# Embedding, state-space mixing and routed experts on one core: the order of every engine's steps given as lists

## The reference, cut to what matters

```python
h = patches(x) @ W_proj + b_proj + pos_emb            # 32 x 36 tokens
h = concatenate([h, weights[positions(x_txt)]])       # 32 x 68 tokens, 256 wide
# attention stand-in: projections, gate, convolution, a linear scan over the 68 tokens, then
out = einsum('blh,dh->bld', y, W_out) + b_out         # y: 512 wide
h = h + layernorm(xn + out, ln_g, ln_b)               # xn = layernorm(h)
# feed-forward: x2 = layernorm(h), top 2 of 4 experts
g = softmax(layernorm(x2, rn_g, rn_b) @ router_w.T)
hid = relu(layernorm(x2 @ w1[e], ln_g[e], ln_b[e]))   # 512 wide
out = sum over the 2 experts of (hid @ w2[e]) * weight
h = h + layernorm(out, on_g, on_b)
```

## Time and profile before

| | |
|---|---|
| median of the runs | 492.49 us |
| the profiled execution: time, span | 492.58 us, 490.8 us |
| from the output projections to the last block (226 to 460 us) | 234 us |
| from there to the end | 31 us |
| granted clock of TensorE, mean | 0.957 |

### The profile page before, as it was taken

How to read it: one execution, slowest core, us unless ns; L and a number is a source line. 1 busy time by engine, 2 the same in 40 slices (tenths; PEclk the granted TensorE clock), 3 DMA queues, 4 the chain that set the end, 5 groups by cost and what they waited for, 6 DMA issues and landing times.

```text
span 490.8 us, 9987 instructions
## 1 busy us (share of the span) xinstructions
PE 431.7 (88%) x3149; PEld 363.0 (74%) x3149; DVE 334.1 (68%) x981; ACT 295.2 (60%) x667; POOL 156.3 (32%) x261
## 2 busy tenths in 40 slices
PE   7879999799899999999989789999999999999400
PEld 5769977567688878787877667888878888888300
DVE  6886576688999325335887877857665666565584
ACT  2854468277966465226654455876786777877351
POOL 6000000000000000002253887764778644553322
PEclk9999999799999999989989999999999999999855
DMA  8982099700039742964411322222322333252252
GB/s 177 190 230 58 33 320 325 230 0 2 1 77 256 183 115 67 240 212 140 140 45 54 100 83 68 98 87 67 109 98 77 109 108 110 75 148 79 94 198 83
DMA packets 58734, 59.94 MB, mean 122 GB/s; under 512 B 25368, under 2 KB 51260, under 8 KB 57404
## 3 DMA queue, kind: packets, MB, share of 16 engines
q1 hardware_dynamic: 54236, 48.68, 37.0%
q0 software_dynamic: 3552, 9.74, 5.3%
q10 hardware_dynamic: 896, 0.89, 0.7%
HBM read 34.50 MB, written 24.80 MB: 121 GB/s over the span
## 4 chain that ended last, share of the span: by engine, by line
PE 57%; DVE 12%; issue 10%; POOL 8%; ACT 8%; DMA 3%; SPq 1%; POOLq 0%; DVEq 0%; ACTq 0%
PE bank L1047 12%; PE bank L884 9%; PE bank L434 8%; PE bank L436 7%; PE bank L435 7%; POOL sorted_x L674 3%; PE bank L1033 3%; PE bank L904 3%; PE bank L958 2%; POOL h L709 1%; DMA expert_y<-ysb,toid 1%; PE bank L1015 1%; DMA got<-expert_y 1%; ACT U L471 1%; DVE spj L1408 1%
## 5 line engine op out<-in xcount | busy, mean ns | idle before, releaser
L1047 PE MATMUL bank<-w,hr 128*128 x320 | 75.8, 380 | 1.1 <-DVE ysb L1670 0.6
L1047 PEld LDWEIGHTS bank<-w,hr 128*128 128x128 f32 x320 | 60.1, 190 | 11.1 <-issue 2.1
L647 POOL MEMSET ones<- 128x128 f32 x1 | 0.2, 209 | 204.9 <-PE bank L919 204.9
L1241 ACT ACTIVATE hr<-bank,gsel 128x128 f32<-128x128 f32 x160 | 59.9, 461 | 0.0
L722 POOL DMA_INDIRECT expert_y<-ysb,toid x40 | 42.8, 1070 | 50.6 <-DVE ysb L1670 30.6
L884 PE MATMUL bank<-Tb,U 68*32 68x68 f32 x1024 | 45.4, 354 | 0.3 <-issue 0.3
L884 PEld LDWEIGHTS bank<-Tb,U 68*32 68x32 f32 x1024 | 40.1, 140 | 3.6 <-issue 3.0
L1655 DVE BATCH_NORM_STATS2 bsth<-bank 128x6 f32<-128x512 f32 x40 | 27.7, 693 | 20.1 <-PE bank L436 19.8
L674 POOL DMA_INDIRECT sorted_x<-x2s,slot x34 | 33.6, 987 | 14.9 <-issue 9.7
L1233 ACT ACTIVATE hn<-bank,nmrh,rsh 128x512 f32<-128x512 f32 x40 | 31.1, 778 | 11.5 <-DVE nmrh L1664 9.9
L434 PE MATMUL bank<-w_hi,bT_hi 128*128 x80 | 35.0, 438 | 0.2 <-issue 0.2
(11 more groups left out here) (304 smaller groups left out, 1169.6 us busy)
## 6 DMA issues: line engine op xcount, KB each, us to landing
Tb<-ssm_kernels SPq DMA_DIRECT2D x16, 680.0 KB, 7.3
sorted_x<-zpad SPq DMA_DIRECT2D x6, 1419.0 KB, 13.3
xg<-sorted_x SPq DMA_DIRECT2D x40, 129.0 KB, 2.1
got<-expert_y SPq DMA_DIRECT2D x17, 256.0 KB, 4.3
XI<-in_x_dram SPq DMA_DIRECT2D x12, 288.0 KB, 5.6
h0r<-h_spill SPq DMA_DIRECT2D x17, 128.0 KB, 2.1
out_dram<-acc SPq DMA_DIRECT2D x17, 128.0 KB
...
```

The lines of the kernel that those rows point to most:

```text
L1047: mm = pe.matmul(bank[second_bank(i)][:, 0:D], hr[:, i % 3, c, :], w2[:, bass.ds(expert[i], 1), c, :].rearrange("p o n -> p (o n)"), start ...
L1241: last = act.activation(hr[:, i % 3, c, :], bank[3 + i % 2][:, c * P:(c + 1) * P], ACT.Relu, scale=gsel[:, i, 0, c:c + 1], bias=gsel[:, i, ...
```

## The change

The numbers and `place_of` are gone. Each engine has a string, one letter for a step; the k-th occurrence of a letter is index k of its kind (`w1s` and all others run upward in index). Operations, waits, buffers and `fill` are the same; every engine has the same set of steps as before in another sequence.

```diff
-        RUN = 0.1
-        HEAD = PARTS[0].stop // 2
-        STARTS = dict(tiles=((-228.34, 36.22), (-51.95, 71.10)), blocks=((49.05, 19.06), (417.37, 19.11)),
-                      sums=((579.34, 113.82), (1443.32, 34.88)))
...
-            "dve": dict(out=-176.0, ln1a=-146.8, ln1b=-131.0, h1a=-113.1, x2=-95.4, c1=-68.1, c2=0.8, lg=-50.7,
...
-            t0, dt = STARTS["sums" if kind in SUMS else "tiles"][int(n >= HEAD)]
-            return t0 + (n - HEAD if n >= HEAD else n) * dt + AT[who][kind] + (late * AT["odd"][kind] if late else 0)
...
-            return sorted(steps, key=lambda s: place_of(who, *s))
+        NAMES = {
+            "pe": dict(y="yT", o="out", x="x2T", l="lgm", r="rank", g="regs", a="b1", b="b2", c="b3", d="b4"),
...
+        STEPS = {
+            "pe": (
+                "yyooyyooyyoxolxyyloxoxlyxlxolyrolxxyllorxyloyxggoylogxylxaolyboraycoaxblxabdcaxbladabclxcbdacbda"
+                "xblcdabcadlbdcracbdcdabcgbdacdacbadbdcabgacbdacdbcbdgacdabacbdacdbcbadcbadcabdacbdadcbcbaddacbca"
...
+            left = {kind: instances(who, kind) for kind in NAMES[who].values()}
+            return [(NAMES[who][step], next(left[NAMES[who][step]])) for step in STEPS[who]]
```

More of the change, by code:

```diff
@@ L330, in build_kernel @@
         BLOCKWISE = ["load", "b1", "b2", "rs", "b3", "b4", "regs"]
-        SUMS = ["gat", "fin", "c1w", "c1", "c1s", "c2"]
-        AT = {
-            "pe": dict(yT=-196.1, out=-183.6, x2T=-64.7, lgm=-52.1, rank=-9.0, b1=-49.5, b2=-29.4, b3=8.6, b4=36.1,
-                regs=-29.9),
-            "act": dict(xb=-73.8, yT=-86.8, x2T=39.6, ln1a=-26.3, h1a=7.4, x2=32.8, c1w=35.2, c1s=70.4, c2=112.5,
-                wts=162.2, w1s=-57.8, b1=56.3, b2=91.7, rs=104.7, b3=124.9),
-            "pool": dict(h0b=-38.0, scat=143.9, h1b=89.4, c2=115.8, table=262.8, b1=97.3, b4=177.0),
-            "sp": dict(h0in=-396.7, load=199.7, gat=184.7, fin=774.5),
-            "dve": dict(out=-176.0, ln1a=-146.8, ln1b=-131.0, h1a=-113.1, x2=-95.4, c1=-68.1, c2=0.8, lg=-50.7,
-                sel=-33.7, rank=-5.0, table=56.5, rel=47.7, wts=211.8, w1s=-153.3, b1=-50.1, b2=-21.6, rs=-12.0,
-                b4=42.9),
-            "odd": dict(h0in=19.9, yT=28.5, xb=24.0, h0b=25.2, out=28.6, x2T=11.6, lgm=7.1, scat=15.3, gat=24.0,
-                fin=35.6, w1s=-435.8)}
@@ L345, in place_of @@
-        def place_of(who, kind, i):
-            late = 0
-            if kind in BLOCKWISE:
-                (t0, dt), n = STARTS["blocks"][block_part(i)], i - FIRST[block_part(i)]
-                return t0 + n * dt + AT[who][kind]
-            if kind == "w1s":
-                n, late = 0, i
-            elif kind == "scat":
-                first_part = group_of(i) < PART0_GROUPS
-                n, late = RG[group_of(i)][-1] // 2, (i - RG[group_of(i)][0]) * (RUN if first_part else 1)
-            elif kind in BY_GROUP:
-                n = RG[i][-1] // 2
-            elif kind in BY_PART:
-                n = PARTS[i].stop // 2 - 1 + i
-            elif kind in BY_TILE:
-                n, late = i // 2, i % 2
-            else:
-                n = i
-            t0, dt = STARTS["sums" if kind in SUMS else "tiles"][int(n >= HEAD)]
-            return t0 + (n - HEAD if n >= HEAD else n) * dt + AT[who][kind] + (late * AT["odd"][kind] if late else 0)
@@ L367, in order @@
-        def order(who):
-            steps = []
-            for kind in AT[who]:
-                count = NK if kind in BLOCKWISE else NT if kind in BY_TILE + ["scat"] else len(RG) if kind in BY_GROUP else E if kind == "w1s" else 2 if kind in BY_PART else len(FB)
-                steps += [(kind, i) for i in range(count) if kind != "regs" or (i - FIRST[block_part(i)]) % 8 == 0]
-            return sorted(steps, key=lambda s: place_of(who, *s))
+        NAMES = {
+            "pe": dict(y="yT", o="out", x="x2T", l="lgm", r="rank", g="regs", a="b1", b="b2", c="b3", d="b4"),
+            "act": dict(h="xb", y="yT", x="x2T", p="ln1a", q="h1a", s="x2", k="c1w", m="c1s", n="c2", t="wts", w="w1s", a="b1", b="b2", e="rs", c="b3"),
+            "pool": dict(h="h0b", s="scat", f="h1b", n="c2", t="table", a="b1", d="b4"),
+            "sp": dict(h="h0in", l="load", g="gat", f="fin"),
+            "dve": dict(o="out", p="ln1a", u="ln1b", q="h1a", s="x2", k="c1", n="c2", l="lg", v="sel", r="rank", t="table", z="rel", j="wts", w="w1s", a="b1", b="b2", e="rs", d="b4"),
+        }
@@ new lines, in there, with instances @@
+        def there(who, kind, i):
+            return kind != "regs" or (i - FIRST[block_part(i)]) % 8 == 0
+        def instances(who, kind):
+            count = NK if kind in BLOCKWISE else NT if kind in BY_TILE + ["scat"] else len(RG) if kind in BY_GROUP else E if kind == "w1s" else 2 if kind in BY_PART else len(FB)
+            return iter([i for i in range(count) if there(who, kind, i)])
+        def order(who):
+            left = {kind: instances(who, kind) for kind in NAMES[who].values()}
+            return [(NAMES[who][step], next(left[NAMES[who][step]])) for step in STEPS[who]]
```

20 lines of the change are left out of this document (added).

## The result

| | before | changed |
|---|---|---|
| median of the runs, same chip | 492.05 us (4 runs, 491.58 to 493.1) | 498.94 us (4 runs, 497.13 to 502.81) |
| ratio | | 1.0126, 95% interval 1.0081 to 1.0172 |
| the profiled execution: time, span | 492.58, 490.8 us | 500.57, 498.8 us |
| end of the scan's last product | 224.4 us | 227.5 us |
| from there to the end of TensorE's last `b4` | 236.0 us | 242.2 us |

Medians and ratios are of the executions in the chip's faster state. The forecast was 493.5 us, 488.0 to 497.5; the result lies outside. The first half is the same work in the same order, yet it is 3.1 us longer in this profile. In the profiles of this study, of both orders, the scan's last product ends anywhere from 223.6 to 230.6 us, and that goes with the granted clock of the first 50 us (1.00 in before, 0.97 here).

What follows compares the result with a forecast made beforehand. The prediction took TensorE's block work to set the pace from 316 to 460 us, with TensorE and VectorE waiting in turn before. -0.5 + 1.1 + 0.9 - 0.6 = +0.9 us on 492.58 gave 493.5 us, range 488.0 to 497.5.

Steps and rivals of the forecast that it cites:

- term 1: 226 to 297 us, ahead of the blocks: gains against a 3.9 us idle at `yT.12`, `b1.0` ending 0.5 us earlier; -0.5 us.
- term 3: 316 to 460 us, the blocks' stage: closer, irregular order and early `table.1`, 2.1 us listed; taken as +0.9, bounds 0 and +4.
- the four stretches: 226 to 297, 297 to 316, 316 to 460 us, and the last 31 us behind TensorE's work: one term each.
- 23.1 - 3.9 - 0.4 + 1.1 = 19.9: From `yT.12` to the end of `b1.0`: old time less old waits and finished `lgm.8`, plus 1.1 us of kept waits.
- Term 2: 297 to 316 us: TensorE waits 0.7 us at `b1.3`, 0.3 at `b3.1`, 0.6 at `b4.1`; +1.1 us.
- The short distances: Blocks' stage: `b3` to `b4` and `b4` to `b4` too close for steps between; 0.4 + 0.2 + 0.2 us, and 0.4 in part 0.
- Term 4: The end behind the blocks: `gat.16` issued later, near 476.4, yet last result at 483.5 instead of 484.1; -0.6 us, -1.5 to +1.5.
- A: Rival, faster: VectorE reaches `rank.1` earlier, half of the 7.9 us lost from 226 to 297 goes; -4, 488.5 us; chance 0.32.
- C: Rival, slower by the clock: it falls behind the `yT.12` wait, `out.12` and its chain take longer; 495.3 us; chance 0.12.
- B: Rival, slower by short distances in the blocks: 0.8 or 1.5 us at close places; 496.6 us; chance 0.20.
- The test of B: TensorE's busy share from 316 to 460 us falling below 0.975 would decide for the rival of short distances.

Runs made afterwards that it cites:

- all_new: The changed kernel's order, built again from the file that holds both orders, against before: +5.6 us by its ratio.
- sums_new: Kernel before with only the end's gathers, stores and sums in the new order: 31.2 us behind the last `b4` instead of 30.4, the time growing with it.

## Why the prediction was wrong

- **The steps that failed**: in term 1, that `regs.0` costs nothing more and the clock stays up behind `yT.12`; in term 3, that `table.1` ahead of `b1.12` costs about 0.5 us, and that the 2.1 us listed come to +0.9.
- **Where the kernel is bound, and the terms**: the four stretches were the right ones. Counted at equal work against the profiled execution of before, they gave +1.3, +1.1, +3.7 (with the last blocks) and -1.3, where I had -0.5, +1.1, +0.9 and -0.6.
- **Term 1**: `yT.12` starts at 279.55 in a profile whose scan ends 3.1 us later, so at 276.4 on the old scale: I had 276.8 (269.0 + 7.7 is 276.7). The wait is 2.25 and not 3.9 us, as TensorE came to it 1.2 us later than I had laid out. The scatters fit too (262.0 to 283.1, I had 261.6 to 283). What failed is "23.1 - 3.9 - 0.4 + 1.1 = 19.9". It took `regs.0` to cost nothing once the table is done; the loads themselves cost 1.2 to 1.5 us. It took the clock as steady; it fell. And it named `b1.0` as its mark, which the new list has ahead of `out.14` and `yT.15`, so it ends 3.0 us earlier while everything around it is later. A mark that is itself moved measures nothing.
- **Term 2** was right in size: +1.1 against 1.1, in waits of 0.65, 0.27 and 0.71 us near 306 to 313. Of the three places only `b1.3` (0.7 forecast, 0.71 measured) is mine; `b3.1` and `b4.1` did not wait, `yT.16` and `out.16` did, so a part of that is luck.
- **Term 3** failed at one of its items: "`table.1` ahead of `b1.12` costs about 0.5". It and `wts.1` cost 2.5 us more than before. I had priced the late `bT` of one block, and neither the next blocks' steps that queue behind 3.8 us of VectorE nor the two table loads of `wts.1`. The short distances, for which I had listed 1.6 us, gave 1.8 on top, mostly at other places than mine (the largest delays in all_new are 0.35 and 0.29 us at `b3.17` and `b3.22`; at block 28, where I had 0.4, there are 0.22). I had cut 2.1 us to 0.9 because waits overlap and the old order has small ones too; from 90 to 200 us of work the old order lost 1.5 us and the new one 5.8.
- **Term 4**: right in size, for the wrong reason. The -1.3 of this profile is partly chance: behind the last `b4` the ten profiles with the whole new end take 29.1 to 30.7 us, 29.8 in the mean, and the seven with the old one 29.9 to 30.5, 30.3 in the mean, so about -0.5. `gat.16` is issued 15.0 us behind the last `b4`, where it was 9.7 before; it takes 4.0 us to landing where I had 3.5, and from there to the last result are 5.3 us where I had 3.5. So the last result is later, 24.3 instead of 23.7 us behind the last `b4`. The gain is in the stores: the span ends 4.8 us behind the last result, where it was 6.7. In the old blocks the new order of the end (sums_new) costs 0.8 us.
- **The rivals**: A is dead. Of C (495.3) the clock did fall behind `yT.12`, together with the register loads that C did not have. Of B (496.6) the short distances came, 1.8 us; `table.1` and `wts.1`, which cost more, are not in B. I had the two as alternatives, with the range at B and half of C. They work in different stretches, so their sum was a case of its own: 493.5 + 3.1 + 1.8 = 498.4 from their own numbers. That this lies beside the 498.94 of the runs is luck: with the first half of before the changed kernel's profile would be 492.6 + 4.8 = 497.4. The test of B, a busy share below 0.975, was badly chosen: the share is 0.980 and the stage still lost 3.7 us.
- **The baseline**: the slow clock ahead of 254 us, 1.8 us, stood in the profile of before and was priced as a gain to be had. Three of the six profiles of the old order without fills there do not have it.
